# Relational weight products in pieces of 512 columns, root product last, one raw weight buffer (four-layer graph network, one core)

## The reference, cut to what matters

```
mean[n, r] = mean over the edges (src -> n) of type r of x[src]
out[n]     = sum over r of mean[n, r] @ W[r]  +  x[n] @ root  +  b
```

## Time and profile before

| what | value |
|---|---|
| three runs, us | 4084.15, 4078.70, 4083.57 (median 4083.57) |
| the profiled execution, us | 4079.27 |
| its span, us | 4077.7 |
| mean granted TensorE clock | 0.948 |
| TensorE matmul busy | 3671.9 us, 90% |
| TensorE weight loads busy | 2824.3 us, 69% |
| VectorE / ScalarE / GpSimd busy | 1660.6 / 884.2 / 630.8 us |

### The profile page before, as it was taken

How to read it: one execution, slowest core, us unless ns; L and a number is a source line. 1 busy time by engine, 2 the same in 40 slices (tenths; PEclk the granted TensorE clock), 3 DMA queues, 4 the chain that set the end, 5 groups by cost and what they waited for, 6 DMA issues and landing times. The chain is left out here.

```text
span 4077.7 us, 55212 instructions
## 1 busy us (share of the span) xinstructions
PE 3671.9 (90%) x19146; PEld 2824.3 (69%) x19146; DVE 1660.6 (41%) x3522; ACT 884.2 (22%) x1785; POOL 630.8 (15%) x706
## 2 busy tenths in 40 slices
PE   4998898989988789999989989999989979779994
PEld 3886454545444559999974469999954448579994
DVE  4886433334242551111113331111223332699996
ACT  0122212212121211111100011111100010168883
POOL 0023555100000000000026520000046500000000
PEclk9988999999999889999999999999999979889997
DMA  1012001010000012333238742333268720100000
GB/s 64 20 54 71 16 8 32 0 39 0 23 0 9 25 50 71 98 96 96 84 125 255 248 154 88 97 96 96 72 191 254 247 96 0 74 9 0 0 0 38
DMA packets 109385, 305.35 MB, mean 75 GB/s; under 512 B 18838, under 2 KB 60355, under 8 KB 109262
## 3 DMA queue, kind: packets, MB, share of 16 engines
q0 software_dynamic: 45312, 191.16, 15.3%
q1 hardware_dynamic: 63950, 112.65, 8.3%
HBM read 225.79 MB, written 77.97 MB: 74 GB/s over the span
## 5 line engine op out<-in xcount | busy, mean ns | idle before, releaser
L508 PE MATMUL bank<-arena 125*125 (+3 forms) x3600 | 762.5, 368 | 0.0
L1013 PE MATMUL bank<-w_hi,xT_hi 128*125 128x384 f32 x2160 | 731.3, 339 | 12.7 <-issue 12.7
L1015 PE MATMUL bank<-w_hi,xT_lo 128*125 128x384 f32 x2160 | 730.1, 338 | 0.0
L1014 PE MATMUL bank<-w_lo,xT_hi 128*125 128x384 f32 x2160 | 729.5, 338 | 0.0
L508 PEld LDWEIGHTS bank<-arena 125*125 125x125 f32 x3600 | 497.6, 190 | 229.3 <-issue 177.2
L610 PE MATMUL bank<-arena 128*125 128x384 f32 x1440 | 514.2, 502 | 52.1 <-DMA arena<-y_d,idx_slot 46.7
L610 PEld LDWEIGHTS bank<-arena 128*125 128x125 f32 x1440 | 254.2, 189 | 306.1 <-issue 146.2
L568 POOL DMA_INDIRECT arena<-y_d,idx_slot x360 | 344.0, 956 | 476.7 <-issue 401.0
L1013 PEld LDWEIGHTS bank<-w_hi,xT_hi 128*125 128x125 f32 x2160 | 401.2, 186 | 13.1 <-issue 13.1
L1333 DVE CAST w_hi<-w_raw 128x2304 fp32r<-128x2304 f32 x34 | 46.3, 1360 | 888.5 <-PE bank L1015 888.5
L1014 PEld LDWEIGHTS bank<-w_lo,xT_hi 128*125 128x125 f32 x2160 | 401.2, 186 | 0.2
(11 more groups left out here) (224 smaller groups left out, 3288.5 us busy)
## 6 DMA issues: line engine op xcount, KB each, us to landing
y_d<-arena SPq DMA_DIRECT2D x320, 187.5 KB
w_raw<-in_L_gnn_W_dram POOLq DMA_DIRECT2D x32, 1152.0 KB, 8.7
arena<-in_L_gnn_W_dram SPq DMA_DIRECT2D x8, 1536.0 KB, 7.8
wadj_d<-arena SPq DMA_DIRECT2D x10, 625.0 KB
arena<-wadj_d SPq DMA_DIRECT2D x1, 6250.0 KB
mask_d<-arena POOLq DMA_DIRECT2D x10, 610.4 KB, 5.3
arena<-mask_d SPq DMA_DIRECT2D x1, 6103.5 KB
arena<-y_d,idx_slot POOLq DMA_INDIRECT x360
```

What stands on the lines that cost most here:

```text
L508: ins = pe.matmul(bank[b][0:P, 0:w], tsc[:, t], f, start=(t == 0), stop=(t == NT - 1))
L1013: pe.matmul(b, xT_hi[:, k, v], w_hi[:, h, k], start=(k == 0), stop=False)
L1014: pe.matmul(b, xT_hi[:, k, v], w_lo[:, h, k], start=False, stop=False)
L1015: ins = pe.matmul(b, xT_lo[:, k, v], w_hi[:, h, k], start=False, stop=(k == KD - 1))
```

## The change

A matrix pair r, r+1 has 1536 columns. They are now cut into three pieces of 512 columns (PW): the first 512 of r; the last 256 of r and the first 256 of r+1; the last 512 of r+1 (`columns`). A loop trip (R // 4 = 2 trips) takes four relations, six pieces (BODY). The root matrix comes after the relations, as one piece of 512 and one of 256 columns. `w_hi` and `w_lo` keep two buffers each, now of 512 columns; `w_raw` has one buffer of 512 columns in place of two of 384. A piece that runs across two relations is loaded by two transfers and each of its products is stored by two. `PRE` goes from 4 to 16. DVE waits for all products of the application, and no longer for the first 20, before it adds the bias.

The diff, cut to its core:

```diff
-    PRE = 4
+    PRE = 16
...
-        w_raw = placed("w_raw", w_at, 2, KD, HD, dt=F32)
-        w_hi = placed("w_hi", w_at + 2 * HW, 2, KD, HD)
-        w_lo = placed("w_lo", w_at + 4 * HW, 2, KD, HD)
+        PW = 512
+        BODY = 6
+        CH = 2 * BODY + 2
+        w_hi = placed("w_hi", w_at, 2, KD, PW)
+        w_lo = placed("w_lo", w_at + 2 * KD * PW, 2, KD, PW)
+        w_raw = placed("w_raw", w_at + 4 * KD * PW, KD, PW, dt=F32)
...
-        y_stage = cut(w_at + 6 * HW, 4, HD, parts=P)
-        bias_row = cut(w_at + 6 * HW + 4 * HD, D, parts=P)
+        y_stage = cut(w_at + 5 * KD * PW, 4, PW, parts=P)
+        bias_row = cut(w_at + 5 * KD * PW + 4 * PW, D, parts=P)
...
-        raw_loaded = [sem(f"raw_loaded{i}") for i in range(2)]
+        raw_loaded = sem("raw_loaded")
...
+        def columns(i):
+
+            r = 2 * (i // 3)
+            return (((r, 0, 0, PW),), ((r, PW, 0, D - PW), (r + 1, 0, D - PW, 2 * PW - D)), ((r + 1, 2 * PW - D, 0, PW),))[i % 3]
+
+        ROOT = ((0, PW), (PW, D))
...
-                with sp.Fori(0, R) as r:
-                    for h in range(2):
+                with sp.Fori(0, R // 4) as b:
+                    for i in range(BODY):
                         for n in range(NT):
-                            i = (h * NT + n) % 4
-                            sp.wait_ge(prod_taken, unit(r * (2 * NT) + ((c * (R + 1) + 1) * 2 + h) * NT + n))
-                            sp.dma_start(y_d[bass.ds(r * N + n * P, P), h * HD:(h + 1) * HD], y_stage[:, i]).then_inc(y_stored[i], 16)
+                            q = i * NT + n
+                            sp.wait_ge(prod_taken, unit(b * (BODY * NT) + (c * CH * NT + q)))
+                            for r, o, at, w in columns(i):
+                                sp.dma_start(y_d[bass.ds(b * (4 * N) + (r * N + n * P), P), o:o + w], y_stage[:, q % 4, at:at + w]).then_inc(y_stored[q % 4], 16)
...
-                for h in range(2):
-                    if c:
-                        pool.wait_ge(w_ready, unit(2 * (R + 1) * c + h - 2))
-                    pool.dma_start(w_raw[:, h], root.rearrange("(k p) c -> p k c", p=128)[:, :, h * HD:(h + 1) * HD]).then_inc(raw_loaded[h], 16)
-                with pool.Fori(0, R) as r:
-                    for h in range(2):
-                        pool.wait_ge(w_ready, unit(r * 2 + ((c * (R + 1) + 1) * 2 + h - 2)))
-                        pool.dma_start(w_raw[:, h], W[bass.ds(r, 1), :, h * HD:(h + 1) * HD].rearrange("o (k p) c -> p (o k) c", p=128)).then_inc(raw_loaded[h], 16)
+                with pool.Fori(0, R // 4) as b:
+                    for i in range(BODY):
+                        pool.wait_ge(w_ready, unit(b * BODY + (c * CH + i - 1)))
+                        for r, o, at, w in columns(i):
+                            pool.dma_start(w_raw[:, :, at:at + w], W[bass.ds(b * 4 + r, 1), :, o:o + w].rearrange("o (k p) c -> p (o k) c", p=128)).then_inc(raw_loaded, 16)
+                for i, (o, end) in enumerate(ROOT):
+                    pool.wait_ge(w_ready, unit(c * CH + 2 * BODY + i - 1))
+                    pool.dma_start(w_raw[:, :, 0:end - o], root.rearrange("(k p) c -> p k c", p=128)[:, :, o:end]).then_inc(raw_loaded, 16)
                 for i in range(4):
-                    pool.wait_ge(y_stored[i], 16 * (R * 2 * NT // 4 * (c + 1) + 1))
+                    pool.wait_ge(y_stored[i], 16 * (2 * (c + 1) * stores(BODY * NT + i) + 1))
...
-                for h in range(2):
+                with act.Fori(0, R // 4) as b:
+                    for q in range(BODY * NT):
+                        act.wait_ge(prod_made, unit(b * (BODY * NT) + (c * CH * NT + q)))
+
+                        act.wait_ge(y_stored[q % 4], b * (16 * stores(BODY * NT + q % 4)) + 16 * (2 * c * stores(BODY * NT + q % 4) + stores(q) + 1))
+                        act.copy(y_stage[:, q % 4], bank[q % 4][0:P, 0:PW]).then_inc(prod_taken, 1)
+                for i, (o, end) in enumerate(ROOT):
                     for n in range(NT):
-                        act.wait_ge(prod_made, unit((c * (R + 1) * 2 + h) * NT + n))
-                        act.copy(node_a[:, n, h * HD:(h + 1) * HD], bank[(h * NT + n) % 4][0:P, 0:HD]).then_inc(prod_taken, 1)
-                with act.Fori(0, R) as r:
-                    for h in range(2):
-                        for n in range(NT):
-                            i = (h * NT + n) % 4
-                            act.wait_ge(prod_made, unit(r * (2 * NT) + ((c * (R + 1) + 1) * 2 + h) * NT + n))
-
-                            act.wait_ge(y_stored[i], (r * 5 + (c * 5 * R + (h * NT + n) // 4 + 1)) * 16)
-                            act.copy(y_stage[:, i], bank[i][0:P, 0:HD]).then_inc(prod_taken, 1)
+                        q = (2 * BODY + i) * NT + n
+                        act.wait_ge(prod_made, unit(c * CH * NT + q))
+                        act.copy(node_a[:, n, o:end], bank[q % 4][0:P, 0:end - o]).then_inc(prod_taken, 1)
...
-                def half_product(m, p, h):
+                def piece_product(m, i, w):
 
                     pe.wait_ge(w_ready, unit(m))
                     for n in range(NT):
-                        pe.wait_ge(prod_taken, unit(p + (n - 4)))
-                        b, v = bank[(h * NT + n) % 4][0:P, 0:HD], slice(n * P, (n + 1) * P)
+                        pe.wait_ge(prod_taken, unit(m * NT + (n - 4)))
+                        b, v = bank[(i * NT + n) % 4][0:P, 0:w], slice(n * P, (n + 1) * P)
                         for k in range(KD):
-                            pe.matmul(b, xT_hi[:, k, v], w_hi[:, h, k], start=(k == 0), stop=False)
-                            pe.matmul(b, xT_hi[:, k, v], w_lo[:, h, k], start=False, stop=False)
-                            ins = pe.matmul(b, xT_lo[:, k, v], w_hi[:, h, k], start=False, stop=(k == KD - 1))
+                            pe.matmul(b, xT_hi[:, k, v], w_hi[:, i % 2, k, 0:w], start=(k == 0), stop=False)
+                            pe.matmul(b, xT_hi[:, k, v], w_lo[:, i % 2, k, 0:w], start=False, stop=False)
+                            ins = pe.matmul(b, xT_lo[:, k, v], w_hi[:, i % 2, k, 0:w], start=False, stop=(k == KD - 1))
                         ins.then_inc(prod_made, 1)
 
-                m0 = c * (R + 1) * 2
-                for h in range(2):
-                    half_product(m0 + h, (m0 + h) * NT, h)
-                with pe.Fori(0, R) as r:
-                    for h in range(2):
-                        half_product(r * 2 + (m0 + 2 + h), r * (2 * NT) + (m0 + 2 + h) * NT, h)
-                pe.wait_ge(prod_taken, unit((m0 + 2 * (R + 1)) * NT - 1))
+                with pe.Fori(0, R // 4) as b:
+                    for i in range(BODY):
+                        piece_product(b * BODY + (c * CH + i), i, PW)
+                for i, (o, end) in enumerate(ROOT):
+                    piece_product(c * CH + 2 * BODY + i, i, end - o)
+                pe.wait_ge(prod_taken, unit((c + 1) * CH * NT - 1))
...
-                def split(m, i, h):
-                    dve.wait_ge(raw_loaded[h], (i + 1) * 16)
+                def split(m, i, arrived, w=PW):
+                    dve.wait_ge(raw_loaded, arrived)
                     dve.wait_ge(prod_made, unit(m * NT + (-NT - 1)))
-                    chain(dve.tensor_copy(w_hi[:, h], w_raw[:, h]))
-                    dve.tensor_tensor(w_lo[:, h], w_raw[:, h], w_hi[:, h].bitcast(F32), op=ALU.subtract).then_inc(w_ready, 1)
-
-                m0 = c * (R + 1) * 2
-                for h in range(2):
-                    if m0 + h >= 2:
-                        split(m0 + h, c * (R + 1), h)
-                    else:
-                        dve.wait_ge(raw_loaded[h], 16)
-                        chain(dve.tensor_copy(w_hi[:, h], w_raw[:, h]))
-                        dve.tensor_tensor(w_lo[:, h], w_raw[:, h], w_hi[:, h].bitcast(F32), op=ALU.subtract).then_inc(w_ready, 1)
-                with dve.Fori(0, R) as r:
-                    chain.loop(r, 2)
-                    for h in range(2):
-                        split(r * 2 + (m0 + 2 + h), r + (c * (R + 1) + 1), h)
-                    chain.end(R, 2)
-                dve.wait_ge(w_ready, unit(m0 + 2 * (R + 1) - 1))
+                    chain(dve.tensor_copy(w_hi[:, i % 2, :, 0:w], w_raw[:, :, 0:w]))
+                    dve.tensor_tensor(w_lo[:, i % 2, :, 0:w], w_raw[:, :, 0:w], w_hi[:, i % 2, :, 0:w].bitcast(F32), op=ALU.subtract).then_inc(w_ready, 1)
+
+                before = c * (2 * landed(BODY - 1) + 32)
+                with dve.Fori(0, R // 4) as b:
+                    chain.loop(b, BODY)
+                    for i in range(BODY):
+                        split(b * BODY + (c * CH + i), i, b * landed(BODY - 1) + (before + landed(i)))
+                    chain.end(R // 4, BODY)
+                for i, (o, end) in enumerate(ROOT):
+                    split(c * CH + 2 * BODY + i, i, before + 2 * landed(BODY - 1) + 16 * (i + 1), end - o)
+                dve.wait_ge(w_ready, unit((c + 1) * CH - 1))
```

(17 more changed lines are left out.)

## The result

The changed kernel takes 4136.26 us (median of four executions, 4125.50 to 4150.00) against 4082.88 (four, 4078.70 to 4084.15): the ratio is 1.0136 with an interval of 1.0114 to 1.0158, **+53 us**. Its profiled execution took 4125.50 us, span 4123.7, 46.2 us more than the 4079.27 of before. The profiled execution is the shortest of its four, so the trace shows less of the loss than the medians do.

What follows compares the result with a forecast made beforehand. TensorE's stream of matmuls bounds the kernel, with a serial chain at its ends. Terms -22.3 + 2.6 + 11.0 + 19.4 = +10.7 us give 4090 us against the profiled execution, 4094 against the median; range 4052 to 4117.

Steps and rivals of the forecast that it cites:

- step 1: Relational products: 720 fewer, wider matmuls per application, the 15.5 ns excess coming once per matmul, gain 22.3 us in both.
- step 2: Start of each application: first split covers 512 columns for 384, +1.3 us each, +2.6 in both.
- step 3: End of each application: root last exposes bias additions, register loads and first pick; +11.0 us (c = 0), +19.4 (c = 1).
- step 4: Products: one raw buffer, four transfers for three pieces and stores in two parts stay covered, cost nothing.
- rival A: fp32r products: excess goes with the columns, gain 0, 4117 us, chance 0.17; against it, a bytes limit would feel weight loads.
- Rival B: Products: weight load is the bound, 175.5 ns its floor, wide matmuls hide it; gain 64.0 us, 4053 us, chance 0.25.
- 107 ns in the earlier trace: Plain float32 passes of 64 columns, each with a weight load, 107 ns apart; held against a weight-load floor of 175.5 ns.
- rivals C and D: Raw pieces late in the products, 4118 us, chance 0.03; chain at the end overlapped after all, 4064 us, chance 0.02.

Runs made afterwards that it cites:

- experiment 5: Kernel before with 64 of 125 stationary columns in 16 of 18 matmuls (c = 0), the same 16 cut into three of 128 columns (c = 1): 5440.18 us.
- Experiments 2: Changed kernel plus 77 idle semaphore instructions in DVE's stream, later code 128 instructions behind its place in the kernel before: 4104.82 us, ratio 1.0055.
- 3: Kernel before plus 51 idle semaphore instructions in DVE's stream, so later code stands where the changed kernel has it: 4115.62 us, ratio 1.0083.
- experiment 4: Changed kernel with 77 idle DVE instructions, root product first again, DVE waiting for its 20 products alone before the bias: 4077.92 us, ratio 0.9988.

## Why the prediction was wrong

It forecast 4094 us with 4052 to 4117 as its range and 0.60 for slower. Slower was right, the size was not: 4136 us, and +46 us on the profiled execution where it had +10.7. Its terms for the profiled execution:

| term | predicted | measured |
|---|---|---|
| step 1, fewer matmuls (first to last product, both streams) | -22.3 | -5.3 |
| step 2, first split, twice | +2.6 | +2.4 |
| step 3, c = 0 | +11.0 | +10.5 |
| step 3, c = 1 | +19.4 | +19.8 |
| step 4 | 0 | one stall of 0.6, in the -5.3 |
| place of the code, fourth layer | none | +13.7 |
| sum | +10.7 | +41.1 of 46 |

As much as the 5 us left was lost before the relational layer: TensorE ends the layer ahead of it 5.3 us later. It does so at 1496.6 to 1497.0 us in the three traces of the kernel before and its two variants, and anywhere from 1498.9 to 1507.4 in the seven of the changed kernel and its variants. Why is open. The other differences (the third layer, the gathered sums, the tail) are 1 to 2 us each and cancel.

Two terms failed: step 1 by 17 us, and the place of the code, which it put at nothing, by 13.7 us in the profiled execution and 27.5 in the medians. Step 1 alone would have left the time within the range (4094 + 17 = 4111 us); the missing term took it out.

**The step that failed in the sum is step 1, "I take once per matmul"**, and it failed by size. With the paces measured (118.5, 175.5, 232.25 ns) an application has 3240 x 0.1755 = 568.6 us before and 2340 x 0.23225 + 180 x 0.1185 = 564.8 after: 3.8 us, 7.6 in both. Of that the streams keep 5.3, as the two dozen matmuls at low clock at their starts are wider now (427 ns for 320, some 1.6 us more in both) and one stall costs 0.6. The three paces lie on one line, 0.444 ns a column plus some 5 ns. The prediction's 2.4 GHz is, in the traces, 384 columns in 320 ns at the granted clock of 0.50 and two bf16 matmuls of 384 columns 0.16 us apart at 1.00: half of 320 is 160 ns, 0.417 ns a column. So of the 15.5 ns that 384 columns have over their columns 10.5 go with the columns and 5 come once: nearly rival A, which got 0.17. The argument for "per matmul" was that the weight load is the same for any width; experiment 5 halves that load's columns and the pace moves by 1 ns at most. What makes the excess grow with the columns isn't shown; by the same run it isn't anything that feels the weight load, which was the point held against rival A. Rival B ("the weight load is the bound") falls as well: it needed 216 ns, and 256 columns, which it left at 175.5, take 118.5. The 107 ns in the earlier trace rows had been read rightly.

**The term that was missing** is the place of the code. The prediction wrote that the stage behind is "only shifted" and costed all code outside the diff at nothing. Experiments 2 and 3 show both directions of it: the shift alone costs the kernel before 31.4 us, and taking it out of the changed kernel gives 27.5 back. Without it the changed kernel stands at +21 to +23 us (4104.82 against 4084.23, ratio 1.0055), and the prediction's +10.7 with step 1 put right by 17.0 is +27.7; the two stages are 25.7 us longer in the trace of experiment 2. That the place of the code is the cause is shown by these runs. That it acts by a refetch of the loop's instructions at each jump rests on the packets (6 against 26 and 27) coming and going with the stalls in five kernels, and on one packet within each stand-still. The profiled execution shows 13.7 us of the 27.5: 8 us for four jumps, and 5 for the 10.2 us at the low clock behind one of them. The other executions spent more time at the low clock (0.936 to 0.939 for 0.941); that it lay behind these jumps is what experiment 3's trace suggests, but they weren't profiled.

**Steps 2 and 3 were right**, each within 0.6 us: 5.14 us for "First split 5.2", 23.33 and 32.54 us for "23.9 and 32.2", and experiment 4 takes 11.1 and 19.9 us back. This was the part of the change that cost most. It was also predictable to the half microsecond, since every link of the new chain had its row.

**Step 4 was right in what it looked at**: the clock and the busy share of the windows show no gap, ACT, DVE and POOL still wait for TensorE, and rivals C and D don't occur. It did not look at TensorE's own program: the trip of the products grew from 360 to 1080 matmuls, each with a weight load, and q8 fetches 25 packets in each application, for 8 and 9. TensorE waited once in the products with nothing named but issue, in c = 1:

```profile
2677.76 0.39 PE L1033 MATMUL bank<-w_lo,xT_hi 128*125 128x512 f32 x1
2678.59 0.50 PE L1034 MATMUL bank<-w_hi,xT_lo 128*125 128x512 f32 x1 [0.44 <-issue]
```

0.83 us for 0.23, the 0.6 us of the table. A packet of q8 ran there from 2676.18 to 2677.06 us; that it caused the wait isn't shown. The chances add up only loosely (a fifth of 0.53 is 0.11, which makes 0.11 for the same and 0.62 for slower, not 0.13 and 0.60); nothing hangs on it. The range was too narrow because every end of it was a pace of TensorE; none of its cases allowed for a cost outside the diff.

## What to carry to other kernels

When a change moves the time and the stage it edits doesn't account for it, compare every stage, look for idle time before the first instruction of a loop trip that is put down to issue, and count the instruction packets; a few idle instructions ahead of the loop tell whether its place is the cause. Time a change with its loops in a good and a bad place before judging it: here the place was worth 27 to 31 us, as much as both exposed chains of step 3 together. And when the same short wait costs 2 us in one trip and 14 in another, look at TensorE's granted clock behind it. Before making matmuls wider, take the pace at two widths; one width can't say which part of the excess comes once.

## What the runs showed of the hardware that was not expected

- A DVE loop of 290 instructions restarts without a wait in its place in the kernel before and 91 and 128 instructions behind it, and after some 2.5 us at 51, there with five packets of 8 KB fetched for each jump back. Four jumps cost 13.7 us in the changed kernel's profiled execution and 35.9 in experiment 3's.
- Most of the difference between these two is TensorE's clock: behind waits of 1.9 to 2.1 us at the jumps the granted clock fell to 0.50 for 3.4 to 23.9 us in some trips and not at all in others, with TensorE busy in these stretches.
- fp32r matmuls at full clock take 0.444 ns a column and some 5 ns, at 256, 384 and 512 columns, with 125 or 64 stationary columns alike (the latter at 384). At the granted clock of 0.50, 384 columns take 320 ns and 512 take 427, 0.833 ns a column in both.
- In experiment 5 a stream of matmuls of 128 columns, each with its weight load, ran through all the products of c = 1 at the granted clock of 0.50 with TensorE 499.72 of 500 us busy, where the same products in 384 columns run at 1.00. The stage took 2245 us for 883.3.
